# One burst of probabilities times values per quad, in the middle of the next quad's scores

## The reference, cut to what matters

```python
qkv = (x @ w_qkv.T).reshape(B, N, 3, H, D).transpose(2, 0, 3, 1, 4)
q, k, v = (qkv[0], qkv[1], qkv[2])
kv = context.reshape(B, N_c, 2, H, D).transpose(2, 0, 3, 1, 4)
extra_k, extra_v = (kv[0], kv[1])
k = jnp.concatenate([extra_k, k], axis=2)
v = jnp.concatenate([extra_v, v], axis=2)
attn = jnp.einsum('bhnd,bhmd->bhnm', q * scale, k).astype(jnp.float32)
attn = jax.nn.softmax(attn, axis=-1).astype(dtype)
out = jnp.einsum('bhnm,bhmd->bhnd', attn, v)
out = out.transpose(0, 2, 1, 3).reshape(B, N, C)
return out @ w_proj.T + b_proj
```

## Time and profile before

| | |
|---|---|
| median of three runs | 556.1 us |
| profiled execution, its own time | 551.65 us |
| its span, first to last instruction | 550.1 us |
| busy: TensorE, VectorE, ScalarE, POOL | 463.2, 355.2, 290.5, 181.5 us |
| mean granted clock of TensorE | 0.919 of full speed |
| exponentials L423 | 384, mean 602 ns |
| reductions L464 | 192, mean 1221 ns |
| pv matmuls L595 | 1536, mean 385 ns |

### The profile page before, as it was taken

How to read it: one execution, slowest core, us unless ns; L and a number is a source line. 1 busy time by engine, 2 the same in 40 slices (tenths; PEclk the granted TensorE clock), 3 DMA queues, 4 the chain that set the end, 5 groups by cost and what they waited for, 6 DMA issues and landing times. The chain is left out here.

```text
span 550.1 us, 10607 instructions
## 1 busy us (share of the span) xinstructions
PE 463.2 (84%) x3467; PEld 273.7 (50%) x3468; DVE 355.2 (65%) x646; ACT 290.5 (53%) x584; POOL 181.5 (33%) x381
## 2 busy tenths in 40 slices
PE   2489999999999999999999987536499999999940
PEld 1255555554555555555555543435266666666630
DVE  7698797786887887887888850669234333333317
ACT  2237776777777777777777776310033333333310
POOL 6141231412312311412300000104446766676630
PEclk9659999999999999999999999655599999999985
DMA  6512224243243242322212100610111111111126
GB/s 176 126 38 68 65 77 109 75 106 89 77 114 95 78 114 75 94 77 62 53 51 62 38 3 0 193 37 0 19 25 41 43 43 35 43 38 38 43 69 181
DMA packets 32254, 38.10 MB, mean 69 GB/s; under 512 B 5604, under 2 KB 20580, under 8 KB 32212
## 3 DMA queue, kind: packets, MB, share of 16 engines
q1 hardware_dynamic: 27252, 30.79, 20.8%
q0 software_dynamic: 2560, 5.25, 3.7%
q10 hardware_dynamic: 2400, 1.51, 1.1%
HBM read 16.58 MB, written 4.72 MB: 39 GB/s over the span
## 5 line engine op out<-in xcount | busy, mean ns | idle before, releaser
L464 DVE TENSOR_REDUCE max_part<-max_ps 128x2 f32<-128x1024 f32 (+1 forms) x192 | 227.2, 1221 | 55.3 <-PE max_ps L562 42.1
L423 ACT ACTIVATE probs<-ring_ps 128x512 f32<-128x512 f32 x384 | 199.7, 602 | 69.8 <-PE ring_ps L585 68.0
L585 PE MATMUL ring_ps<-blocks,keys 64*128 64x512 f32 x384 | 144.9, 461 | 2.9 <-ACT probs L423 2.6
L595 PE MATMUL pv_ps<-probs,value_cols 128*32 128x256 f32 x1536 | 102.6, 385 | 0.0
L562 PE MATMUL max_ps<-keys,blocks 64*128 64x512 f32 x256 | 85.8, 455 | 8.6 <-DMA blocks<-masked 6.6
L1019 DVE TENSOR_TENSOR hidden<-up_ps,silu 128x512 f32<-128x512 f32 x40 | 27.7, 692 | 82.0 <-PE up_ps L1109 79.8
L585 PEld LDWEIGHTS ring_ps<-blocks,keys 64*128 64x128 f32 x384 | 64.8, 186 | 31.6 <-ACT probs L423 28.4
L339 POOL CAST maxes<-rowmax 128x8 fp32r<-128x8 f32 x32 | 6.3, 198 | 173.0 <-DVE rowmax L471 173.0
L912 ACT ACTIVATE hiddenT<-at_ps 128x512 f32<-128x512 f32 x40 | 23.9, 597 | 74.7 <-PE at_ps L1126 66.2
L595 PEld LDWEIGHTS pv_ps<-probs,value_cols 128*32 128x32 f32 x1536 | 40.2, 109 | 36.6 <-issue 10.9
L562 PEld LDWEIGHTS max_ps<-keys,blocks 64*128 64x128 f32 x256 | 41.4, 195 | 33.9 <-issue 22.4
(11 more groups left out here) (148 smaller groups left out, 459.0 us busy)
## 6 DMA issues: line engine op xcount, KB each, us to landing
keys<-parts SPq DMA_DIRECT2D x96, 96.0 KB
blocks<-masked SPq DMA_DIRECT2D x93, 64.0 KB
ctx_v_sb<-ctx_v_dram SPq DMA_DIRECT2D x8, 256.0 KB, 2.9
gate<-gateT_dram SPq DMA_DIRECT2D x8, 256.0 KB, 2.7
up<-upT_dram SPq DMA_DIRECT2D x8, 256.0 KB, 2.7
y_in<-pick_outs SPq DMA_DIRECT2D x8, 256.0 KB, 4.9
raw<-ctx_kT_dram SPq DMA_DIRECT2D x7, 256.0 KB, 2.7
h_rows<-h SPq DMA_DIRECT2D x4, 256.0 KB, 4.9
```

What stands on the lines that cost most here:

```text
L423: act.activation(probs[par][:, k, PAIR * a:PAIR * (a + 1)], bank("exp", s * XUNITS + u)[:].rearrange("p (g n) -> p g n", n=N), ACT.Exp).th ...
L464: vec.reduce_max(out, bank, axis=AX.X).then_inc(max_done, 1)
L585: pe.matmul(ps[:], keys[rows, t, k * P:(k + 1) * P], blocks[rows, t], start=True, stop=True)\
L595: mm = pe.matmul(pv_ps[ROWS * g:ROWS * (g + 1), 0:N], value_cols[:, t, k, g, :], probs[q % 2][:, k, g, :], start=(k == 0), stop=(k == KT - 1))
```

## The change

All six key tiles of a quad's pv go in one burst, after group 2 of the next step. All other work of TensorE stands there too: first the transposes of x, keys and queries, transposes of attention, projection and values, whichever the step has, then the output transposes (now of the quad two before), then the burst, and behind it, ahead of group 3, the transposes of the maxima. ScalarE takes their copies between exponentials 5 and 6. VectorE normalises the quad two before, after its third reduction. Loops run two steps longer. The transposes of x are now in the step with r = 0, keys and queries in r = 1, transposes of attention in r = 2, projection and values in r = 3; before, they were at r = 1, 2, 0, and 1 and 2.

```diff
@@ -159,24 +159,27 @@
         block = ctx.enter_context(nc.Block())
 
         def steps(step):
-            for s in range(-2, QUADS + 2):
+            for s in range(-2, QUADS + 4):
                 step(s, *divmod(s, T))
 
         has_scores = lambda s: 0 <= s < QUADS
 
+        xT_at = lambda c: T * (c - 2)
+        keys_at = lambda c: T * (c - 2) + 1 if c > 1 else 2 * c - 4
+        values_at = lambda c: T * (c - 2) + 3
+        attnT_at = lambda b: T * (b + 1) + 2
+        proj_at = lambda b: T * (b + 1) + 3
+
         turns = [("xT", 0), ("kq", 0), ("v", 0), ("xT", 1)]
-        for s in range(-2, QUADS + 2):
+        for s in range(-2, QUADS + 4):
             b, r = divmod(s, T)
-            later = 0 <= b < B - 2
-            turns += [("exp", s * XUNITS + u) for u in range(2) if has_scores(s)]
-            turns += [("proj", b - 1)] if r == 1 and b >= 1 else [("kq", b + 2)] if r == 2 and b + 2 < B else []
-            turns += [("exp", s * XUNITS + u) for u in range(2, 4) if has_scores(s)]
+            turns += [("exp", s * XUNITS + u) for u in range(6) if has_scores(s)]
+            turns += [("xT", c) for c in range(2, B) if xT_at(c) == s] + [("kq", c) for c in range(B) if keys_at(c) == s]
+            turns += [("attnT", c) for c in range(B) if attnT_at(c) == s] + [("proj", c) for c in range(B) if proj_at(c) == s]
+            turns += [("v", c) for c in range(1, B) if values_at(c) == s]
+            turns += [("out", s - 2)] if 2 <= s <= QUADS + 1 else []
             turns += [("max", s + 1)] if has_scores(s + 1) else []
-            turns += [("exp", s * XUNITS + u) for u in range(4, 8) if has_scores(s)]
-            turns += [("out", s - 1)] if 1 <= s <= QUADS else []
-            turns += [("exp", s * XUNITS + u) for u in range(8, XUNITS) if has_scores(s)]
-            turns += [("attnT", b - 1)] if r == 0 and b >= 1 else [("xT", b + 2)] if r == 1 and later else \
-                [("v", b + 2)] if r == 2 and b + 2 < B else []
+            turns += [("exp", s * XUNITS + u) for u in range(6, XUNITS) if has_scores(s)]
         turn = {unit: n for n, unit in enumerate(turns)}
         taken = {"exp": (exp_done, 1), "max": (maxT_copied, 1), "out": (out_done, 1), "attnT": (attnT_copied, 1),
                  "proj": (proj_done, 1), "xT": (xt_copied, 1), "kq": (kq_copied, 2), "v": (v_copied, 1)}
@@ -402,9 +405,19 @@
             def step(s, b, r):
                 par = s % 2
                 for u in range(XUNITS):
-                    if u == 4:
-                        if r == 2 and b + 2 < B:
-                            copy_keys_queries(b + 2)
+                    if u == 6:
+                        if r == 0 and 0 <= b < B - 2:
+                            copy_xT(b + 2)
+                        for c in range(1, B):
+                            if keys_at(c) == s:
+                                copy_keys_queries(c)
+                        if r == 2 and b >= 1:
+                            act.wait_ge(attnT_filled, b)
+                            wait_for(act, proj_filled, b - 1)
+                            act.activation(attnT[:], bank("attnT", b - 1)[:, 0:QT * P].rearrange("p (q n) -> p q n", n=P),
+                                           ACT.Copy).then_inc(attnT_copied, 1)
+                        if r == 3 and b + 2 < B:
+                            copy_values(b + 2)
                         if 1 <= s <= QUADS:
                             act.wait_ge(pv_filled, s)
                             wait_for(act, out_filled, s - 1)
@@ -422,15 +435,6 @@
                         act.wait_ge(exp_filled, s * XUNITS + u + 1)
                         act.activation(probs[par][:, k, PAIR * a:PAIR * (a + 1)],
                                        bank("exp", s * XUNITS + u)[:].rearrange("p (g n) -> p g n", n=N), ACT.Exp).then_inc(exp_done, 1)
-                if r == 0 and b >= 1:
-                    act.wait_ge(attnT_filled, b)
-                    wait_for(act, proj_filled, b - 1)
-                    act.activation(attnT[:], bank("attnT", b - 1)[:, 0:QT * P].rearrange("p (q n) -> p q n", n=P), ACT.Copy)\
-                       .then_inc(attnT_copied, 1)
-                if r == 1 and 0 <= b < B - 2:
-                    copy_xT(b + 2)
-                if r == 2 and b + 2 < B:
-                    copy_values(b + 2)
 
             steps(step)
 
@@ -513,7 +517,7 @@
                 for w in range(MUNITS):
                     if has_scores(s + 2):
                         reduce_unit(s + 2, w)
-                    if w == 1 and r == 1 and b >= 1:
+                    if w == 2 and r == 3 and b >= 1:
                         vec.wait_ge(proj_filled, b)
                         vec.wait_ge(bias_added, b)
                         tiles = m.x[:, QT * (b - 1):QT * b, :]
@@ -522,8 +526,8 @@
                            .then_inc(proj_done, 1)
                     if w == 1 and r == 0 and 0 <= b < B - 2:
                         normalize_x(b + 2)
-                    if w == 3 and 1 <= s <= QUADS:
-                        normalize(s - 1)
+                    if w == 2 and 2 <= s <= QUADS + 1:
+                        normalize(s - 2)
                 if has_scores(s + 2):
                     row_maxima(s + 2)
 
@@ -631,33 +635,30 @@
 
             def step(s, b, r):
                 for i in range(GROUPS):
-                    if i == 1:
-                        if r == 1 and b >= 1:
-                            project_out(b - 1)
-                        if r == 2 and b + 2 < B:
-                            project_keys_queries(b + 2)
-                    if i == 2 and has_scores(s + 1):
+                    if i == 3 and has_scores(s + 1):
                         transpose_maxima(s + 1)
                     for a in range(2):
                         if has_scores(s + 2):
                             max_half(s + 2, i, 1 - a)
                         if has_scores(s):
                             exp_unit(s, 2 * i + a)
-                    if i == 3 and 1 <= s <= QUADS:
-                        transpose_out(s - 1)
-                    if i == 5:
-                        if r == 0 and b >= 1:
+                    if i == 2:
+                        if r == 0 and 0 <= b < B - 2:
+                            transpose_x(b + 2)
+                        for c in range(1, B):
+                            if keys_at(c) == s:
+                                project_keys_queries(c)
+                        if r == 2 and b >= 1:
                             transpose_attention(b - 1)
-                        if r == 1 and 0 <= b < B - 2:
-                            transpose_x(b + 2)
-                        if r == 2 and b + 2 < B:
+                        if r == 3 and b >= 1:
+                            project_out(b - 1)
+                        if r == 3 and b + 2 < B:
                             project_values(b + 2)
-                    if i == 1 and has_scores(s - 1):
-                        for k in (4, 5):
-                            pv_tile(s - 1, k)
-                    if i in (3, 5) and has_scores(s):
-                        for k in (i - 3, i - 2):
-                            pv_tile(s, k)
+                        if 2 <= s <= QUADS + 1:
+                            transpose_out(s - 2)
+                        if has_scores(s - 1):
+                            for k in range(KT):
+                                pv_tile(s - 1, k)
 
             steps(step)

```

## The result

The changed kernel takes 630.35 us (median of 4 runs, 627.45 to 631.37; a fifth took 622.37), the kernel before 556.75 beside it. The ratio is 1.128 (95% interval 1.120 to 1.136), 73.6 us more. Forecast were 591 us and a range to 608. The profiled execution is 627.45 us against 551.65.

What follows compares the result with a forecast made beforehand. Scores were taken to run at the readers' pace, with pv bursts as catch-up time. Stage +32, start +3 and end +0.4 gave +35 us: profiled 551.65 to 587, plus 4.4 to the median, 591; range 574 to 608.

Steps and rivals of the forecast that it cites:

- the readers' pace: Score groups on TensorE go as fast as ScalarE and VectorE read their banks; reductions 1.13 us apart, stage +32 us.
- The burst: 48 pv records on TensorE in one run: busy 2.79 us, next kind of work 2.72 after its start.
- the score stretch: Six score groups between breaks; those held by VectorE start 2.05, 3.18, 4.31 and 5.78 us after group 3.
- The kinds of quad: Quad lengths by other work at the break: quiet 9.8 us, x 11.2, keys and queries 10.9, attention 10.4, projection and values 11.1.
- The stage: Thirty quads between transposed maxima 1 and 31: 319 us against 287.55 before, +32.
- the distance of profile and median: Median shown was 4.4 us above the profiled execution; the same distance was added to the forecast 587.
- the rival of ScalarE alone: Score stretch paced only by ScalarE: quiet quad 9.2 us, +12 to +24, about 574 us; chance 0.12.
- The new wait: At the break, transposes of x wait for VectorE's normalising, ready at 7.4 us; quads with x take 11.2.
- DMA of the maxima: Maxima land by 2.3 us, needed at 3.18, 0.9 of room; rival that they land late: about 617 us, chance 0.08.
- Gathering the other work: Each piece of other work at the one break was priced there; only the transposes of x got a new wait.
- the clock falls: Rival: TensorE's short waits lower the granted clock, break of 4 us becomes 8, about 710 us; chance 0.02.
- The drain on switching: Switching TensorE's tiling drains it; fewer switches gain 0.6 us a quad; rival of array gain 538 us, chance 0.03.

Runs made afterwards that it cites:

- experiment 1: Changed kernel plus one small unused matmul after each of the five score groups that another group follows: 591.7 us, ratio 1.064 to the kernel before.
- experiment 3: Changed kernel with VectorE's reductions reading half of each bank: 560.04 us with small matmuls behind the score groups, 562.15 without; ratios 1.007 and 1.009 to the kernel before.
- experiment 7: Changed kernel with small matmuls behind score groups, and VectorE's normalising of x one step earlier: 586.6 us against 591.7.
- experiment 5: Changed kernel with pv put back to three bursts of two key tiles, other work still gathered after group 2: 553.48 us, ratio 0.992 to the kernel before.
- experiment 4: Kernel before with only pv changed to one burst of six key tiles, and ScalarE's pv copy behind exponential 5: 611.62 us, ratio 1.097.

## Why the prediction was wrong

The direction and the mechanism of the waits were right, and nearly the size of the readers' pace; the clock, whose cost the sum put at nothing, was wrong.

- *The burst* (2.72 us) and *the score stretch* came out within 0.13 us at each step of the quad above. The kinds of quad, forecast and at the high level of the clock (experiment 1): quiet 9.8 and 9.70; x 11.2 and 10.89; keys and queries 10.9 and 10.61; attention 10.4 and 10.29; projection and values 11.1 and 10.78. The stage: 319 and 316.33. That the whole is 591.7 in experiment 1, where 591 was forecast, is in part luck: the stage and the distance of profile and median (0.9 us, not 4.4) came out smaller than in the sum, and the experts 6 us longer.
- *What goes first at the readers' pace*: VectorE, as forecast against the rival of ScalarE alone (27.6 us, experiment 3). ScalarE's own pace was set too slow: the sum took 0.515 us from one exponential to the next, and nine in a row in experiment 3 (without small matmuls) take 4.54 with 0.60 for the last, so 0.49. That is why a quiet quad at ScalarE's pace is 9.05 and not the 9.2 of that rival.
- *The new wait* of x: real, 0.6 us in each such quad (experiment 7).
- *DMA of the maxima*: not the bound; none of TensorE's waits in the stage is put down to a DMA. The prediction's reading of the earlier trace rows passes over the 33 GB/s of 329.5 to 330.0; the slices of 10 and 6 are the 8 KB of the maxima, and the rest goes by the instruction queue, which the same view lists with 0.02 MB.
- *Gathering the other work*: taken as neutral but for the wait; by itself it gains (experiment 5), because it does away with the waits of the transposes of the maxima for a bank, which the sum let stand. With the one long burst it gains nothing and goes with a lower clock.
- **The step that failed** is the clock: the sum kept it at 1.00, so at no cost, and the rival "the clock falls" was put at 0.02 and at the price of a clock low all the time. It said "the steady stage at 1.00 speaks against it". That row was of a TensorE busy 8.62 of 8.70 us; the sum let it wait in pieces of 0.3 to 0.7 us (it turned out to be busy 8.50 of 10.28), which no row of the steady stage shows. The clock did fall, for part of the time: 0.84 in the mean, which cost 36.8 us of the 69.8 in attention. No row of before gave that price. The rows with TensorE held by VectorE group after group are those of the start, in a stretch at 0.59; but experiment 4 has the same six reductions in a row in the same stretch with the clock at 1.00, so these waits did not make the 0.59:

```profile
20.80:46.00 25.20, 21.11 (x78) 12.56 (x80) 22.11 (x24) 8.73 (x19) 6.69 (x14) 1.00 0.23 59
```

- *The Trainium skill*, TensorE: Matmul & The Clock Gate, "A second HAM failure mode: psum-queue depth-cycling", tells of a TensorE that idles briefly and often between groups while cycling through banks, and of a clock that goes back and forth. The prediction cited it and gave it next to no weight. The changed kernel does this: 0.84 in the mean of the stage, at 1.00 in one quad and 0.73 in another.
- *The drain on switching*, which the Trainium skill states (TensorEngine Tiling (Array Packing), Key Properties), was the case for one burst. No row shows a drain as such, but a price per burst there is. Six bursts, with the most switches, are the fastest here all the same: a burst of one tile takes 0.57 us to the next group, six of them 3.4, against 2.72 for one burst of six. The 0.7 us more cost nothing in sum, since the waits that they replace were longer: TensorE's idle time in the stage is 0.2 us in place of 47.1.
- *Experts, and distance of profile and median*: 4.4 us were carried over from before; the changed kernel's profile is 2.9 below its median. The experts, forecast at their old lengths, took 5.9 us more, at a lower clock.

Open: what exactly in the pattern of waits decides whether the clock falls in a given quad. The experiments show that the mean share of work does not decide it, and that with the waits for reductions shortened or gone it stays up. No run varied the length of the waits by itself, and none shows why experiment 4, whose matmuls waited 6.8 us for reductions and 21.3 for a bank, is at 0.91.

## What to carry to other kernels

A burst that empties no buffer starves the readers once they have read what they hold: here three banks, 1.5 us, against a burst of 2.7. But fitting within that is not enough: with the other work gathered, bursts of six, three, two and one tile gave 630.35, 571.54, 553.48 and 531.6 us, and the one of three tiles is busy just those 1.5. Where a forecast adds waits to TensorE, the clock of the steady state that it leaves says nothing about the clock with the waits: give the fall a chance and a price between none and all the time, and test it early, as experiment 1 does. And when a change loses, try the opposite direction: half of this one was good, and with bursts cut to one tile it is 4.5% faster than the kernel before.

## What the runs showed of the hardware

- More work made a kernel faster: five matmuls a quad, one behind each group of scores, took 39 us off, and placed at the break they added 31.
- The granted clock of the stage was 0.99 and 0.84 in two kernels whose TensorE was busy 89% of it.
- The experts, unchanged, took 50.2 and 141.0 us in one profile and 53.3 and 143.8 in the other, at clocks 0.53 and 0.98, and 0.50 and 0.96. In experiment 5, faster than before and with its attention stage at 0.99, they took as long as in the changed kernel. So the stage behind a change can move by some 6 us that are not the change's own.
- The same six reductions in a row, with TensorE held by them, stood in a stretch at 0.59 in one kernel and at 1.00 in another.
